# The last tile of a quantised feed-forward in chunks, with four buffers for its output rows and residual rows

## The reference

```
x   = x + tanh(g_xattn) * cross_attention(layernorm(x), ctx)      # causal, 16 heads of 32
x   = x + tanh(g_ffn) * ffn(layernorm(x))
ffn: gate, up = split(quant(x) @ quant(w_gate_up).T)              # 512 -> 2 x 1408
     h  = silu(gate) * up
     hq = round(h / step) * step,  step = max|h| of the row / 127 # one step for each token's row of 1408
     return hq @ quant(w_down).T                                  # 1408 -> 512
```

## Time and profile before

| What | Value |
|---|---|
| Time, median of 3 runs | 771.4 us (769.3 to 772.21) |
| Time of the profiled execution | 771.57 us |
| Its span in the trace | 769.7 us |
| PE busy | 717.2 us, 93% of the span |
| DVE busy | 621.4 us, 81% |
| POOL busy | 580.1 us, 75% |
| ACT busy | 412.9 us, 54% |

### The profile page before, as it was taken

How to read it: one execution, slowest core, us unless ns; L and a number is a source line. 1 busy time by engine, 2 the same in 40 slices (tenths; PEclk the granted TensorE clock), 3 DMA queues, 4 the chain that set the end, 5 groups by cost and what they waited for, 6 DMA issues and landing times.

```text
span 769.7 us, 17015 instructions
## 1 busy us (share of the span) xinstructions
PE 717.2 (93%) x5345; PEld 515.8 (67%) x5345; DVE 621.4 (81%) x1894; ACT 412.9 (54%) x657; POOL 580.1 (75%) x766
## 2 busy tenths in 40 slices
PE   2488899999999999999999999999999999999993
PEld 2477788798788888888887886755544444444441
DVE  4644867888879789789789878779999999999982
ACT  5433675775765775765765753455534443443440
POOL 5433776887877977977977965668888888888884
PEclk9676999999999999999999999999999999999998
DMA  7685767869769679779779559974846755665665
GB/s 236 154 221 139 203 174 185 203 193 222 199 174 248 169 197 247 174 198 219 201 201 240 141 138 218 244 186 80 162 119 149 160 129 143 153 148 133 146 145 161
DMA packets 137919, 137.59 MB, mean 179 GB/s; under 512 B 90317, under 2 KB 99815, under 8 KB 137703
## 3 DMA queue, kind: packets, MB, share of 16 engines
q1 hardware_dynamic: 136768, 135.97, 71.5%
q10 hardware_dynamic: 1063, 0.54, 0.4%
HBM read 40.24 MB, written 25.31 MB: 85 GB/s over the span
## 4 chain that ended last, share of the span: by engine, by line
PE 60%; issue 13%; POOL 13%; DVE 6%; DMA 5%; ACT 2%; SPq 1%; POOLq 0%; ACTq 0%; DVEq 0%
PE psum L1344 11%; PE psum L1366 10%; PE psum L1408 9%; POOL hidden L664 5%; PE psum L1626 5%; PE psum L1297 5%; PE psum L1382 4%; PE psum L1295 4%; POOL y L678 4%; PE psum L1354 3%; PE psum L1331 3%; DMA x1b<-x_scratch 2%; DMA heads<-nmT 2%; POOL hq L671 2%; PE psum L1636 2%
## 5 line engine op out<-in xcount | busy, mean ns | idle before, releaser
L995 DVE CUSTOM_DVE_ANT_0 junk<-psum,mask 128x128 f32<-128x128 f32 (+1 forms) x512 | 153.7, 353 | 68.9 <-PE psum L1297 66.7
L1626 PE MATMUL psum<-w1q,xqb 128*128 128x512 bf16 (+1 forms) x768 | 158.1, 361 | 1.2 <-DVE u L1036 1.2
L664 POOL TENSOR_TENSOR hidden<-hidden 128x512 f32<-128x512 f32 (+1 forms) x96 | 112.6, 1188 | 28.9 <-ACT hidden L931 28.6
L775 ACT ACTIVATE prob<-psum 128x768 f32<-128x768 f32 x128 | 103.5, 809 | 52.7 <-PE psum L1384 51.4
L1626 PEld LDWEIGHTS psum<-w1q,xqb 128*128 128x128 bf16 x768 | 74.4, 98 | 80.1 <-DVE u L1036 1.6
L936 ACT ACTIVATE hidden<-hidden,round_bias,hinv 128x1408 f32<-128x1408 f32 x32 | 49.9, 1560 | 113.7 <-DVE hinv L1250 113.7
L522 POOL TENSOR_SCALAR_AFFINE_SELECT prob<-prob 128x512 f32<-128x512 f32 x128 | 81.4, 639 | 32.0 <-ACT prob L775 30.9
L530 POOL TENSOR_TENSOR prob<-prob 128x256 f32<-128x256 f32 x128 | 98.1, 772 | 6.5
L1636 PE MATMUL psum<-w2q,hqT 128*128 128x512 bf16 x352 | 82.6, 385 | 6.2 <-DMA hqT<-hq 6.2
L1344 PE MATMUL psum<-xT_hi,wq_hi 128*128 128x256 f32 x256 | 75.8, 296 | 10.0 <-POOL xT_lo L537 10.0
L1297 PE MATMUL psum<-heads 96*128 96x256 f32 x256 | 78.0, 341 | 0.0
(11 more groups left out here) (116 smaller groups left out, 1798.5 us busy)
## 6 DMA issues: line engine op xcount, KB each, us to landing
heads<-q_hi SPq DMA_DIRECT2D x128, 128.0 KB, 4.3
heads<-k_hi SPq DMA_DIRECT2D x128, 128.0 KB, 4.4
xln<-x_dram SPq DMA_DIRECT2D x16, 512.0 KB, 5.4
heads<-q_lo SPq DMA_DIRECT2D x64, 128.0 KB, 4.0
heads<-k_lo SPq DMA_DIRECT2D x64, 128.0 KB, 3.6
x<-x_dram SPq DMA_DIRECT2D x16, 512.0 KB, 4.2
x_scratch<-x SPq DMA_DIRECT2D x16, 512.0 KB, 4.0
x1b<-x_scratch SPq DMA_DIRECT2D x32, 256.0 KB, 3.4
```

The costliest lines, as they stand in the source:

```text
L664: pool.tensor_tensor(up[t % 3][:, o], gate[t % 3][:, o], up[t % 3][:, o], ALU.mult).then_inc(f["prod_done"], 1)
L775: act.activation(prob[:, g % 2, pair % 2, 0:CAUSAL // P].rearrange("p k h q -> p h k q"), psum[:, 2:4, 0:CAUSAL].rearrange("p h (k q) -> p ...
L995: dve.tensor_tensor_reduce(junk[:, n % 2, 0:w], psum[:, h % 2, cols], m, 1.0, LOWEST, ALU.add, ALU.max, mx[:, X % 2, t, h:h + 1]).then_inc ...
L1626: last = pe.matmul(psum[:, bank, 0:w], xqb[:, t % 4, k, :], w1q[:, k, half * I + o:half * I + o + w], start=(k == 0), stop=(k == KH - 1))
```

## The change

It touches the code from tile 31 (`LAST`) on, and two buffer counts.

- `y` and `x1b` have four buffers each instead of two, with four semaphores each for loads and stores. `weigh_out(t)` waits for the store of tile t - 4, `load_x1(t)` for `add_residual(t - 4)`.
- `run` calls `tile(t)` for tiles 6 to 30 only, and then a new function `closing()`, which each engine has for itself.
- In `closing`, DVE scales all three chunks of tile 31 before `hidden_step(30)`, and ACT does all three `silu` of tile 31 before `magnify(30)`.
- Of the products of tile 31, POOL does chunk 0 and DVE chunks 1 and 2 (`late_product`).
- Tile 31's scaling and quantisation go by chunks: ACT magnifies chunks 0 and 1, DVE chunk 2; POOL quantises chunk 0, DVE chunks 2 and 1 (`late_chunks`).
- Instead of one `turn(31)` there are three transposing DMAs, in the order chunk 2, 0, 1 (3, 4 and 4 blocks), and `down(31)` becomes three groups of matmuls, each behind its own transfer.
- The residual of tile 31 is added on DVE instead of POOL. SP issues `load_x1` for tiles 28, 29 and 30 ahead of `turn(30)`, and `load_x1(31)` ahead of the three transposing DMAs.

The core of the diff:

```diff
-        x1b = keep("x1b", [P, 2, H], F32)
+        x1b = keep("x1b", [P, 4, H], F32)
...
-        y = keep("y", [P, 2, H], F32)
+        y = keep("y", [P, 4, H], F32)
...
             ending()
-            for t in range(STARTED, NT + 4):
+            for t in range(STARTED, LAST):
                 tile(t)
+            closing()
...
                 def load_x1(t):
                     if is_tile(t):
-                        wait_for(sp, f["out_done"], t - 1)
+                        wait_for(sp, f["out_done"], t - 3)
...
+                def turn_chunk(c):
+                    sp.wait_ge(f[f"last_hq{c}"], 1)
+                    sp.wait_ge(f["d_done"], LAST - 3)
+                    o, w = CHUNKS[c]
+                    sp.dma_start_transpose(hqT[:, LAST % 4, o // P:(o + w) // P], hq[:, LAST % 2, o:o + w]).then_inc(f[f"last_moved{c}"], DMA)
+
+                def closing():          # SP
+                    load_x1(LAST - 3)
+                    load_x1(LAST - 2)
+                    load_x1(LAST - 1)
+                    turn(LAST - 1)
+                    store_out(LAST - 4)
+                    load_x1(LAST)
+                    for c in (2, 0, 1):
+                        turn_chunk(c)
+                    for t in range(LAST - 3, LAST):
+                        store_out(t)
+                    sp.wait_ge(f["last_out"], 1)
+                    sp.dma_start(out_tiles[LAST], y[:, LAST % 4]).then_inc(f[f"stored{LAST % 4}"], DMA)
...
+                def closing():          # POOL
+                    product(LAST, 0)
+                    quantise_hidden(LAST - 1)
+                    add_residual(LAST - 4)
+                    pool.wait_ge(f["last_hm"], 1)
+                    pool.wait_ge(f[f"ht_moved{LAST % 2}"], DMA * (LAST // 2))
+                    o = slice(CHUNKS[0][0], CHUNKS[0][0] + CHUNKS[0][1])
+                    pool.tensor_scalar(hq[:, LAST % 2, o], up[LAST % 3][:, o], 1.0, -ROUND, ALU.mult, ALU.add).then_inc(f["last_hq0"], 1)
+                    for t in range(LAST - 3, LAST):
+                        add_residual(t)
...
+                def closing():          # ACT
+                    for c in range(3):
+                        silu(LAST, c)
+                    magnify(LAST - 1)
+                    magnify_chunk(0)
+                    magnify_chunk(1)
...
                 def weigh_out(t):
                     if is_tile(t):
                         dve.wait_ge(f["d_done"], t + 1)
-                        wait_for(dve, f[f"stored{t % 2}"], DMA * (t // 2))
+                        wait_for(dve, f[f"stored{t % 4}"], DMA * (t // 4))
...
+                def late_chunks():      # DVE
+                    u2 = up[LAST % 3][:, CHUNKS[2][0]:I]
+                    u1 = up[LAST % 3][:, CHUNKS[1][0]:CHUNKS[2][0]]
+                    dve.wait_ge(f["hinv"], LAST + 1)
+                    dve.tensor_scalar(u2, u2, hinv[:, LAST % 2:LAST % 2 + 1], ROUND, ALU.mult, ALU.add).then_inc(f["last_c2"], 1)
+                    dve.wait_ge(f["last_c2"], 1)
+                    dve.wait_ge(f[f"ht_moved{LAST % 2}"], DMA * (LAST // 2))
+                    dve.tensor_scalar(hq[:, LAST % 2, CHUNKS[2][0]:I], u2, 1.0, -ROUND, ALU.mult, ALU.add).then_inc(f["last_hq2"], 1)
+                    weigh_out(LAST - 3)
+                    dve.wait_ge(f["last_hm"], 2)
+                    dve.tensor_scalar(hq[:, LAST % 2, CHUNKS[1][0]:CHUNKS[2][0]], u1, 1.0, -ROUND, ALU.mult, ALU.add).then_inc(f["last_hq1"], 1)
+
+                def closing():          # DVE
+                    for c in range(3):
+                        gate_part(LAST, c, 2 * c)
+                        up_part(LAST, c, 2 * c + 1)
+                    hidden_step(LAST - 1)
+                    weigh_out(LAST - 4)
+                    late_product(1)
+                    late_product(2)
+                    hidden_step(LAST)
+                    late_chunks()
+                    weigh_out(LAST - 2)
+                    weigh_out(LAST - 1)
+                    weigh_out(LAST)
+                    dve.wait_ge(f["y_done"], LAST + 1)
+                    dve.wait_ge(f[f"x1_loaded{LAST % 4}"], DMA * (LAST // 4 + 1))
+                    dve.tensor_tensor(y[:, LAST % 4, :], y[:, LAST % 4, :], x1b[:, LAST % 4, :], ALU.add).then_inc(f["last_out"], 1)
...
+                def closing():          # PE
+                    gates_and_ups(LAST)
+                    for t in range(LAST - 3, LAST):
+                        pe.wait_ge(f["y_done"], t - 1)
+                        down(t)
+                    pe.wait_ge(f["y_done"], LAST - 1)
+                    first = True
+                    for c in (2, 0, 1):
+                        pe.wait_ge(f[f"last_moved{c}"], DMA)
+                        for j in range(CHUNKS[c][0] // P, (CHUNKS[c][0] + CHUNKS[c][1]) // P):
+                            last = pe.matmul(psum[:, 6 + LAST % 2, :], hqT[:, LAST % 4, j, :], w2q[:, j, :], start=first,
+                                             stop=(c == 1 and j == (CHUNKS[1][0] + CHUNKS[1][1]) // P - 1))
+                            first = False
+                    last.then_inc(f["d_done"], 1)
```

More of the change, by code:

```diff
@@ L235, in is_tile, with run @@
             return 0 <= t < NT
-        def run(slot, ending, tile):
+        def run(slot, ending, tile, closing):
             for b in range(FIRST, B - 2):
@@ L299, in load_x1 @@
                     if is_tile(t):
-                        wait_for(sp, f["out_done"], t - 1)
+                        wait_for(sp, f["out_done"], t - 3)
                         sp.wait_ge(s["x1_stored"], DMA * (t // ST + 1))
-                        sp.dma_start(x1b[:, t % 2], x1_scratch[t]).then_inc(f[f"x1_loaded{t % 2}"], DMA)
+                        sp.dma_start(x1b[:, t % 4], x1_scratch[t]).then_inc(f[f"x1_loaded{t % 4}"], DMA)
                 def store_out(t):
@@ L444, in tile @@
                     store_out(t - 4)
-                run(slot, ending, tile)
-                for p in range(2):
-                    sp.wait_ge(f[f"stored{p}"], DMA * NT // 2)
+                def turn_chunk(c):
[16 more added lines that the diff above has]
+                    sp.dma_start(out_tiles[LAST], y[:, LAST % 4]).then_inc(f[f"stored{LAST % 4}"], DMA)
+                run(slot, ending, tile, closing)
+                for p in range(4):
+                    sp.wait_ge(f[f"stored{p}"], DMA * NT // 4)
             @block.gpsimd
@@ L676, in add_residual @@
                         pool.wait_ge(f["y_done"], t + 1)
-                        pool.wait_ge(f[f"x1_loaded{t % 2}"], DMA * (t // 2 + 1))
-                        pool.tensor_tensor(y[:, t % 2, :], y[:, t % 2, :], x1b[:, t % 2, :],
+                        pool.wait_ge(f[f"x1_loaded{t % 4}"], DMA * (t // 4 + 1))
+                        pool.tensor_tensor(y[:, t % 4, :], y[:, t % 4, :], x1b[:, t % 4, :],
                                            ALU.add).then_inc(f["out_done"], 1)
@@ L685, in tile @@
                     add_residual(t - 4)
-                run(slot, ending, tile)
+                def closing():
[8 more added lines that the diff above has]
+                        add_residual(t)
+                run(slot, ending, tile, closing)
             @block.scalar
@@ L943, in tile, with magnify_chunk @@
                     silu(t, 2)
-                run(slot, ending, tile)
+                def magnify_chunk(c):
+                    o = slice(CHUNKS[c][0], CHUNKS[c][0] + CHUNKS[c][1])
+                    act.wait_ge(f["hinv"], LAST + 1)
+                    act.activation(up[LAST % 3][:, o], up[LAST % 3][:, o], ACT.Identity,
+                                   scale=hinv[:, LAST % 2:LAST % 2 + 1], bias=round_bias[:, 0:1]).then_inc(f["last_hm"], 1)
+                def closing():
[4 more added lines that the diff above has]
+                    magnify_chunk(1)
+                run(slot, ending, tile, closing)
             @block.vector
@@ L1237, in hidden_step @@
                         p, q = t % 2, t % 4
-                        dve.wait_ge(f["prod_done"], 3 * t + 3)
+                        dve.wait_ge(f["prod_done"], 3 * t + (3 if t < LAST else 1))
+                        if t == LAST:
+                            dve.wait_ge(f["last_prod"], 2)
                         wait_for(dve, f["hstep"], t)
@@ L1638, in down, with gates_and_ups @@
                         last.then_inc(f["d_done"], 1)
-                def tile(t):
[L1641 to L1646, removed]
+                def gates_and_ups(t):
+                    for c in range(3):
+                        pe.wait_ge(f["a_done"], 3 * (t - 1) + c + 1)
+                        gate_up(t, c, 0, 2 * c)
+                        pe.wait_ge(f["c_done"], 3 * (t - 1) + c + 1)
+                        gate_up(t, c, 1, 2 * c + 1)
+                def tile(t):
+                    gates_and_ups(t)
                     wait_for(pe, f["y_done"], t - 4)
                     down(t - 3)
-                run(slot, ending, tile)
+                def closing():
```

(2 more changed lines are left out.)

21 lines of the change are left out of this document (14 added, 7 removed).

## The result

The changed kernel takes 766.45 us (median of 7 runs, 765.02 to 770.18) against 771.4 us (769.3 to 772.78, 7 runs): ratio 0.9942, 95% interval 0.9919 to 0.9964, that is 2.8 to 6.2 us less. The forecast was 766.0, in a range of 764.4 to 769.5. The profiled execution has a span of 766.3 us and a time of 768.32.

The account below looks back on a forecast made before the run. TensorE bounds the equal tiles, so only the tail behind the last gate_up could be won. Buffers 2.4, PE 2.5 and addition 0.56 shorten the span by 5.4 us: 766.0 against 771.4, range 764.4 to 769.5.

Parts of the forecast that it names:

- the likeliest case: The forecast itself: TensorE's clock does not fall, PE ends at 760.0, time 766.0; chance 0.42.
- the first rival: TensorE's granted clock falls before down(30), losing about 1.7 us: PE ends at 761.2, time 767.2; chance 0.26.
- The buffers: Four buffers for y and x1b remove weigh_out(31)'s store wait and the load wait: 2.4 us less, nothing else changed.
- The addition on DVE: Tile 31's last residual addition takes 0.70 on DVE instead of 1.26 on POOL: 0.56 us less.
- The moved scaling: Chunk 2's scaling ahead of hidden_step(30) delays magnify(30) by 1.16 us, but hidden; turn(30) leaves 1.5 us earlier, at 750.7.
- The maximum: DVE's maximum of tile 31 starts at 749.6, 1.3 us earlier than 750.92, with products on DVE.
- The chunk operations: DVE's scaling and quantising of tile 31's chunk 2 take 0.4 to 0.5 us each, ready at 753.0.
- SP's queue: SP sets tile 31's transfer times: turn(30) holds it 1.38 us, chunks leave at 753.5, 754.85 and 756.2, last 0.1 earlier.
- Landing of the chunks: Tile 31's chunk transfers take 2.9 us to land, overlapping: at 756.4, 757.75 and 759.1.
- the two last rivals: Transposing DMAs queue one behind another: at 3.6 us each, time 771.2, chance 0.09; at 4.5 each, 773.9, chance 0.04.
- a sign of being wrong: Profile signs against the forecast on SP's transfers: issues 1.8 us apart, landings of chunks over 4 us.
- PE at the full clock, ending at 760.0: down(30) and the chunk groups run at about 0.21 us per matmul; PE ends at 760.0 instead of 762.53, 2.5 us less.

Follow-up runs that it names:

- e1: Kernel before with four buffers for y and x1b and nothing else; median 771.89 us, ratio 0.9995 to the kernel before.
- e2: Kernel before with four buffers and the x1b loads in the changed kernel's early places on SP; median 769.24 us, ratio 0.9972 to the kernel before.
- e10: Changed kernel with tile 31's residual added on POOL again instead of DVE; median 768.9 us, ratio 0.9969 to the kernel before.
- e12: Changed kernel with all three products of tile 31 on POOL again; median 766.81 us, ratio 0.9941 to the kernel before.
- e3: Changed kernel with two buffers for y and x1b again, x1b loads of tiles 29 to 31 spread behind turn(30); 768.11 us, ratio 0.9958 to the kernel before.
- e8: Changed kernel with x1b loads 30 and 31 behind the chunk transfers and 13 extra matmuls straight behind down(29); 766.86 us, ratio 0.9933 to the kernel before.
- e6: Changed kernel with the x1b loads of tiles 30 and 31 behind the three chunk transfers on SP; 767.0 us, ratio 0.9947 to the kernel before.
- e9: Changed kernel again, unchanged, for a second profile and more times; median 768.38 us, ratio 0.9953 to the kernel before.
- e4: Changed kernel with 14 extra matmuls before down(30), behind the wait for weigh_out(28); median 769.34 us, ratio 0.9957 to the kernel before.
- e5: Changed kernel with 16 extra matmuls straight behind down(29), ahead of the wait for weigh_out(28); median 766.13 us, ratio 0.9937 to the kernel before.
- e11: Changed kernel with one transfer for tile 31 and 16 extra matmuls straight behind down(29); median 766.04 us, ratio 0.9930 to the kernel before.
- e7: Changed kernel with tile 31 turned by one 11-block transposing DMA instead of three; median 767.91 us, ratio 0.9948 to the kernel before.

## Why the prediction came out right, step by step

- **The time** was met, 766.0 against 766.45, but not by the likeliest case. The trace has the figures of the first rival, the fall of the clock: PE's end forecast at 761.2 (T0 + 21.3) in that case, measured T0 + 21.9, and a time forecast of 767.2. The profiles of the changed kernel gained 3.9 and 2.8 us from T0 on, the medians 4.95 and 3.9. Forecast were 5.4. That the first median lies so near is luck within a spread of 5 us between runs.
- **The buffers, 2.4 us "with nothing else changed"**, is the step that failed: e1 gained nothing. The second half of the edit, SP's early loads, carries it (e2, 2.5 us behind PE). I had counted the waits for loads as waits for a buffer; they were waits for SP's queue, where each load stands behind a store that waits for an addition. In the sum the term was still right, because the change has both halves: 3.2 us less behind PE, against 3.0 forecast for buffers and addition. Early loads without the second pair of buffers were not tried; with two buffers each would hold SP until the addition two tiles ahead of it is done.
- **The addition on DVE**, 0.56: 0.6 by e10.
- **The moved scaling** (hidden, `turn(30)` 1.5 earlier): measured 12.34 - 10.81 = 1.5. But it is not DVE's taking over of products that pays; all but 0.4 of it stays without that (e12). By the order of time it is the silu of tile 31 ahead of `magnify(30)`, with the scaling that they need; no run moved these alone.
- **The maximum** of tile 31: forecast T0 + 9.7, measured 9.6. **The chunk operations** on DVE: 0.42, 0.36 and 0.43, where 0.4 to 0.5 were taken. The Trainium skill's port rule (SBUF — State Buffer, Who interferes with whom) left no mark on DVE here, and could hardly: the first of them started 0.10 us before POOL's addition ended, in e12 0.17 before, and took 0.42 both times. POOL bears the mark in all eleven profiles with chunks. Its addition that started about 0.01 us behind DVE's last chunk quantisation took 1.54 instead of 1.26, which agrees with the rule. It is off the path.

```profile
753.14 0.43 DVE L1335 TENSOR_SCALAR hq<-hidden 128x512 bf16<-128x512 f32 x1
...
753.15 1.54 POOL L701 TENSOR_TENSOR y<-y,x1b 128x512 f32<-128x512 f32 x1
```

- **The casts of the earlier trace rows** say more than the prediction took from them. The four of the 16 beside which no POOL instruction was running at their start took 0.29 to 0.30 us. Where one had 0.32 us left to run the cast took 0.47, with 0.45 left 0.59 or 0.60, with 0.52 left 0.67, with 0.79 left 0.95. The price on DVE is the rest of POOL's instruction less about 0.15, and POOL's 0.28 is the rest of DVE's 0.43 less 0.15.
- **SP's queue**: mis-sized. I took 1.38 for `turn(30)`; it was 2.37, and the chunk issues began at T0 + 14.5 instead of 13.6. The last chunk left at T0 + 17.1, not 0.1 earlier than the whole tile before (16.4) but 0.7 later. Without three loads just ahead it was 1.27 to 1.41 and 3.5 to landing (e2, e3, e8), in e6 1.71 and 4.1; with them 2.0 to 2.5 and 4.3 to 6.8 (eight profiles). In these eight `turn(30)` landed 1.3 to 1.6 us behind the last of the three loads, late or not. Its lateness goes with theirs: I had put it at 0.5 (754.8 instead of 754.3); it was 1.0 in the first profile and 3.3 in e10.
- **Landing of the chunks**, forecast 2.9: the view of the line of the changed kernel shows 2.4 to 3.0, issues 1.21 apiece. Three transposing DMAs in a row didn't queue up; the two last rivals fall. In other runs single chunks took up to 4.7 (e9), which the prediction had named as a sign of being wrong ("landings of chunks over 4").

```profile
L454 SPq DMA_TRANSPOSE hqT<-hq x3: 1184/1211/1217, 754.9 to 757.5; - x3
...
DMA to landing us min/median/max: 2.4/2.5/3.0
```

- **PE at the full clock, ending at 760.0**: the other step that failed. Of the 2.5 us that the sum gives to PE, 0.7 came in the first profile and none in the second. Of the ten profiles whose gap was left empty, nine met the lower clock (e4's late filling met it too); in all three with the gap filled at once it held (e5, e8, e11). e5 shows the price: with the gap filled PE ends 1.3 and 2.4 us earlier than in the two profiles of the changed kernel, although tile 30 landed later. With the clock held the forecast's 20.1 for PE was nearly reached (20.6).

What was not measured: the split into three transfers apart from everything else. At the lower clock `down(30)` hides either way: in the changed kernel the third chunk landed at T0 + 19.5, when `down(30)` ended, and one transfer would have been there at 18.7 (e7, e11). At the full clock e7 waited 0.98 for the one transfer and e11 not at all. In times, e7 and the changed kernel can't be told apart. Open is also why the loads ahead of `turn(30)` took 7.3 us once, and why the clock held once in a gap that was left empty. The three versions with the gap filled at once are the fastest from T0 on, 24.7, 24.9 and 25.4, at ratios of 0.9937, 0.9933 and 0.9930; next to 0.9942 and 0.9953 for the changed kernel, with intervals of 0.002 to 0.003 to either side, no version is shown to beat it.

## What to carry to other kernels

A second pair of buffers does nothing while the load still stands, in a queue written out by hand, behind a store that waits for work; move the issue as well, and look what it then stands in front of. Price a tail's matmuls at both levels of the clock if PE idles before them, and give the fallen clock the larger chance. Compare tails from a common event, not from the start of the span, when the front scatters by more than the effect.

## What the hardware showed beyond that

- The granted clock fell in gaps of 3.06 us (e3) and 3.57 (e6), and held in one of 3.86 (e7); the length of the gap alone doesn't settle it. The same kernel then ran 11 matmuls in 4.04 us once and in 4.85 another time.
- With three 256 KB loads issued shortly before it, a transposing DMA held SP for 2.0 to 2.5 us instead of 1.3 to 1.4 and landed later. The two don't grow together: 2.06 came with a landing of 6.8 (e10), 2.33 with 4.4 (e7). The landing follows the last load, 1.3 to 1.6 us behind it.
- In the kernel before a plain load issued right behind a transposing DMA held SP for 0.69 to 0.76 us, behind a store for 0.38 or 0.39; these are the two ends of the earlier trace rows. In the changed kernel three loads in a row held it for 1.39 together, and the prediction's 0.43 for the store behind `turn(30)` and 0.74 for the load behind that came out as 0.71 and 0.38.
